# Carries between partitions: from a mended row in DRAM to a product on PE that is added to the gathered run ends, in a four-layer graph network

## The reference

```python
# gat, gatv2, agnn: for each node, over the run of its edges
e = logits(src_features[src], dst_features[dst])
mx = segment_max(e, dst)
ex = exp(e - mx[dst])
out = segment_sum(ex * features[src], dst) / segment_sum(ex, dst)
# cheb0, cheb1: a plain sum over the run
agg = segment_sum((x * Dinv)[src], dst) * Dinv
```

## Time and profile before

| what | us |
|---|---|
| median of 3 runs | 2605.67 (2603.86 to 2609.76) |
| the profiled execution, its time | 2609.88 |
| its span, first to last instruction | 2608.2 |
| PE busy | 1944.9 (75%) |
| DVE busy | 1824.3 (70%) |
| POOL busy | 1740.8 (67%) |
| ACT busy | 894.1 (34%) |

### The profile page before, as it was taken

One profiled execution on the slowest core, in us unless ns is written; L12 is line 12 of the kernel. 1 busy time (PEld: TensorE's weight loads), 2 busy tenths in 40 slices (PEclk: granted clock), 3 DMA queues, 4 the chain that ended last, 5 costly groups with the idle time before them and its releaser, 6 DMA issues.

```text
span 2608.2 us, 51551 instructions
## 1 busy us (share of the span) xinstructions
PE 1944.9 (75%) x20425; PEld 1698.5 (65%) x20425; DVE 1824.3 (70%) x4953; ACT 894.1 (34%) x861; POOL 1740.8 (67%) x1625
## 2 busy tenths in 40 slices
PE   2778775559995399956888956588888888589990
PEld 1778775349995399955888952255555555589990
DVE  7699999145553255542799874488888888599975
ACT  0377765125443154432344534100000000144542
POOL 7777774437775677765667753577777777467773
PEclk7888887569998699975999985699999999799995
DMA  6233332112221122211412213311111111232221
GB/s 234 57 125 124 117 111 89 56 39 65 76 66 35 46 65 77 65 36 50 151 51 64 65 36 143 124 49 50 50 49 50 50 50 47 90 125 65 66 60 21
DMA packets 83703, 194.91 MB, mean 75 GB/s; under 512 B 30960, under 2 KB 49816, under 8 KB 79746
## 3 DMA queue, kind: packets, MB, share of 16 engines
q1 hardware_dynamic: 31650, 139.14, 14.8%
q0 software_dynamic: 51936, 54.27, 10.8%
HBM read 107.92 MB, written 85.39 MB: 74 GB/s over the span
## 4 chain that ended last, share of the span: by engine, by line
POOL 25%; DVE 14%; issue 13%; PE 9%; DMA 2%; ACT 1%; DVEq 0%; POOLq 0%; ACTq 0%
POOL edges_d L600 17%; PE ps L712 7%; POOL rows L600 6%; DVE edges_d L1287 3%; DVE bigT L1354 2%; PE ps L853 2%; POOL starts_dram L603 2%; POOL agg L600 1%; DVE agg L1079 1%; DVE smallT L1079 1%; DVE aggn L1079 1%; DVE prod L1637 1%; DVE logit L1643 1%; DVE prod L1640 1%; DVE rows L1107 1%
## 5 line engine op out<-in xcount | busy, mean ns | idle before, releaser
L712 PE MATMUL ps<-nodes,edges_d 125*128 125x160 bf16 x7140 | 499.4, 234 | 92.4 <-ACT edges_d L895 88.7
L712 PEld LDWEIGHTS ps<-nodes,edges_d 125*128 125x128 bf16 x7140 | 498.2, 98 | 93.7 <-ACT edges_d L895 91.1
L600 POOL DMA_INDIRECT edges_d<-tab_y_dram,attr x425 | 432.1, 1017 | 180.7 <-issue 129.2
L600 POOL DMA_INDIRECT rows<-tab_cheb_dram,src_i x374 | 412.1, 1102 | 174.7 <-issue 112.2
L712 PE MATMUL ps<-nodes,aggn 125*128 125x180 bf16 (+2 forms) x3546 | 395.2, 244 | 122.1 <-DVE rows L1107 63.1
L759 PE MATMUL ps<-edges_d,scan 125*125 125x480 bf16 x1700 | 363.7, 371 | 106.3 <-DVE edges_d L1737 106.3
L1107 DVE COPY_PREDICATED rows<-picks,ps 125x192 f32<-125x192 uint16 (+4 forms) x880 | 353.5, 403 | 82.1 <-issue 41.6
L759 PEld LDWEIGHTS ps<-edges_d,scan 125*125 125x125 bf16 x1700 | 227.8, 137 | 243.2 <-DVE edges_d L1737 110.4
L712 PE MATMUL ps<-nodes,agg 125*128 125x180 bf16 (+2 forms) x3564 | 336.1, 243 | 63.0 <-DVE rows L1107 63.0
L712 PEld LDWEIGHTS ps<-nodes,aggn 125*128 125x128 bf16 x3546 | 292.4, 101 | 128.7 <-DVE rows L1107 62.8
L712 PEld LDWEIGHTS ps<-nodes,agg 125*128 125x128 bf16 x3564 | 283.6, 101 | 68.5 <-DVE rows L1107 54.7
(11 more groups left out here) (334 smaller groups left out, 3146.5 us busy)
## 6 DMA issues: line engine op xcount, KB each, us to landing
src<-srcT_dram SPq DMA_DIRECT2D x70, 437.5 KB
scan_dram<-scan SPq DMA_DIRECT2D x17, 1700.0 KB
scan_dram<-scan SPq DMA_DIRECT2D x34, 425.0 KB
tab_y_dram<-edges_d SPq DMA_DIRECT2D x5, 2880.0 KB, 8.2
scanD_dram<-scan SPq DMA_DIRECT2D x34, 400.0 KB
starts_dram<-scan SPq DMA_DIRECT2D x2, 3400.0 KB, 14.0
edges_d<-tab_y_dram,attr POOLq DMA_INDIRECT x425, 2.6
src<-srcT_dram SPq DMA_DIRECT2D x18, 375.0 KB
```

The source lines that it names most:

```text
L600: pool.indirect_dma_start(o, None, table, bass.IndirectOffsetOnAxis(index, 0)).then_inc(s, SLOT)
L712: ins = pe.matmul(columns_ps[:, i, 0:PICKS * w], hots_[b][lot][:, i * NP:i * NP + P], parts_[:, part, at:at + PICKS * w], start=(lot == 0 ...
```

## The change

The carry no longer goes through DRAM in the four passes with at most one head. In the set-up, each partition's first destination node gets its place among the nodes: `first_row_of` (125x125) is one where the partition's first node lies on that node partition, and only for the first partition of those that begin with the same node; `first_col_of` (125x25) is one in that node's column. At the end of a pass DVE spreads the carry over the 25 columns by a product with `first_col_of` (800 elements in a row in cheb, 25 x 36 = 900 in gatv2 and agnn), and three products on PE with `first_row_of` bring it to the nodes' partitions, into three banks of PSUM. In cheb0 and cheb1 POOL gathers the run ends at once, without `local`, and `block_in` adds PSUM to `agg`. In gatv2 and agnn POOL still gathers `local` first (DVE takes the maximum from it), then gathers the run ends at once; DVE sets two factors per node (`node_keep`), and `block_in` scales the gathered sums and maximum and adds what PE brought, in four instructions. "gat", with four heads, mends its rows in DRAM as before. `no_carry_pq` is computed in each softmax pass, after DVE has released a product on PE, and not in the set-up; the set-up has a further iota on POOL and nine further instructions on DVE.

```diff
...
+    MC = HG + 3
...
+        def mend_rows(c):
+            return tab[0:NP, :, :].rearrange("p j c -> p (j c)")[:, 0:J * c].rearrange("p (j c) -> p j c", c=c)
+
+        def mend_ps(m, c):
+
+            return ps[0:NP, 3 + m // 2, m % 2 * LS * c:(m % 2 + 1) * LS * c].rearrange("p (j c) -> p j c", c=c)
...
+                pool.iota(cross[:, 0:NP], [[1, NP]], base=0, channel_multiplier=0,
+                          allow_small_or_imprecise_dtypes=True).then_inc(consts_made, 1)
+                pool.wait_ge(consts_made, 11)
...
-                    gather(local[:, 0:C], scan_dram, mend_get_i[:, 0:1], local_in)
-                    pool.wait_ge(vec_for_pool, vec_pool.up())
-                    scatter(scan_dram, mend_put_i[:, 0:1], mended[:, 0:C], E - 1)
-                    pool.wait_ge(scattered, put.at())
+                    if heads:
+                        gather(local[:, 0:C], scan_dram, mend_get_i[:, 0:1], local_in)
+                    if heads > 1:
+                        pool.wait_ge(vec_for_pool, vec_pool.up())
+                        scatter(scan_dram, mend_put_i[:, 0:1], mended[:, 0:C], E - 1)
+                        pool.wait_ge(scattered, put.at())
                     for j in range(J):
                         gather(agg[:, j, 0:C], scan_dram, end_i[:, j:j + 1], agg_in[j // LS])
...
+                def carry_to_nodes(c):
+
+                    pe.wait_ge(vec_for_pe, operand.up())
+                    for at in range(0, J, 2 * LS):
+                        n = min(2 * LS, J - at) * c
+                        ins = pe.matmul(ps[0:NP, 3 + at // (2 * LS), 0:n], first_row_of[:, :],
+                                        tab[0:NP, :, :].rearrange("p j c -> p (j c)")[:, at * c:at * c + n],
+                                        start=True, stop=True)
+                    ins.then_inc(pe_for_vec, 1)
...
                         pe.matmul(ps[0:NP, 6, 0:C], carry_qp[:, :], scan[0:NP, 0, (L - 1) * C:L * C],
                                   start=True, stop=True).then_inc(pe_for_vec, 1)
+                        carry_to_nodes(D)
                         return
...
+                    if heads == 1:
+                        carry_to_nodes(MC)
...
-                vec.tensor_scalar(no_carry_pq[:, :], carry_pq[:, :], -1.0, BIG, ALU.add, ALU.mult)
...
+                row_, col_, later = (place_of[:, i:i + 1] for i in range(3))
+                steps = cross[:, 0:NP]
+                again = cross[:, NP:2 * NP]
+                vec.tensor_scalar(row_, ends[:, 0:1], 1.0 / J, -(J // 2) / J, ALU.mult, ALU.add).then_inc(vec_done, 1)
+                settle()
+                vec.tensor_scalar(row_, row_, ROUND, None, ALU.add).then_inc(vec_done, 1)
+                settle()
+                vec.tensor_scalar(row_, row_, -ROUND, None, ALU.add).then_inc(vec_done, 1)
+                settle()
+                vec.scalar_tensor_tensor(col_, row_, -float(J), ends[:, 0:1], ALU.mult, ALU.add).then_inc(vec_done, 1)
+                settle()
+                vec.scalar_tensor_tensor(again, firsts, ends[:, 0:1], before_qp[0:NP, 0:NP], ALU.is_equal, ALU.mult)\
+                    .then_inc(vec_done, 1)
+                settle()
+                vec.tensor_reduce(later, again, X_AXIS, ALU.max).then_inc(vec_done, 1)
+                settle()
+                vec.tensor_scalar(later, later, -1.0, 1.0, ALU.mult, ALU.add).then_inc(vec_done, 1)
+                settle()
+                vec.tensor_scalar(first_row_of[:, :], steps, row_, later, ALU.is_equal, ALU.mult)
+                vec.tensor_scalar(first_col_of[:, :], steps[:, 0:J], col_, None, ALU.is_equal)
...
+                    vec.tensor_scalar(no_carry_pq, carry_pq[:, :], -1.0, BIG, ALU.add, ALU.mult)
...
+                    else:
+                        vec.tensor_copy(mended[0:NP, HG:HG + 1], cross[:, NP:NP + 1])
+                        vec.tensor_copy(mended[0:NP, HG + 1:HG + 2], small[:, 1, 0:1])
+                        vec.memset(mended[0:NP, HG + 2:MC], 1.0).then_inc(vec_for_pe, 1)
                     vec.wait_ge(pe_for_vec, pe_n.up())
                     vec.tensor_copy(crossT[:, 0:heads, :],
                                     ps[0:NP, 7, 0:heads * NP].rearrange("p (h q) -> p h q", h=heads))\
                         .then_inc(vec_for_pe, 1)
                     vec.wait_ge(pe_for_vec, pe_n.up())
+                    agg_n.up(LS * SLOT)
+                    if heads == 1:
+                        vec.tensor_copy(mended[0:NP, 0:HG], ps[0:NP, 6, 0:HG]).then_inc(vec_done, 1)
+                        settle()
+                        carry_to_nodes(mended[0:NP, 0:MC], MC)
+                        for m in range(J // LS):
+                            made = mend_ps(m, MC)
+                            vec.tensor_scalar(node_keep[:, 0, m * LS:(m + 1) * LS], made[:, :, HG + 2], -1.0, 1.0,
+                                              ALU.mult, ALU.add).then_inc(vec_done, 1)
+                        own.up(J // LS - 1)
+                        settle()
+                        for m in range(J // LS):
+                            js = slice(m * LS, (m + 1) * LS)
+                            vec.tensor_tensor(node_keep[:, 1, js], node_keep[:, 0, js], mend_ps(m, MC)[:, :, HG],
+                                              ALU.add).then_inc(vec_done, 1)
+                        own.up(J // LS - 1)
+                        settle()
+                        return
                     vec.tensor_tensor(mended[0:NP, 0:heads * HG], mended[0:NP, 0:heads * HG],
                                       ps[0:NP, 6, 0:heads * HG], ALU.add).then_inc(vec_for_pool, 1)
-                    agg_n.up(LS * SLOT)
-
-                def block_in(m):
+
+                def carry_to_nodes(carry, c):
+
+                    vec.tensor_tensor(mend_rows(c), over(first_col_of[:, :], c),
+                                      carry.unsqueeze(1).broadcast_to([NP, J, c]), ALU.mult).then_inc(vec_for_pe, 1)
+                    vec.wait_ge(pe_for_vec, pe_n.up())
+
+                def block_in(m, heads=None):
 
                     vec.wait_ge(agg_in[m], agg_n.at())
+                    js = slice(m * LS, (m + 1) * LS)
+                    if heads == 0:
+                        vec.tensor_tensor(agg[0:NP, js, 0:D], agg[0:NP, js, 0:D], mend_ps(m, D), ALU.add)\
+                            .then_inc(vec_done, 1)
+                        settle()
+                    if heads == 1:
+                        vec.tensor_tensor(agg[0:NP, js, 0:HG], agg[0:NP, js, 0:HG], over(node_keep[:, 1, js], HG),
+                                          ALU.mult)
+                        vec.tensor_tensor(agg[0:NP, js, HG], agg[0:NP, js, HG], node_keep[:, 0, js], ALU.mult)\
+                            .then_inc(vec_done, 1)
+                        settle()
+                        vec.tensor_tensor(agg[0:NP, js, 0:HG], agg[0:NP, js, 0:HG], mend_ps(m, MC)[:, :, 0:HG], ALU.add)
+                        vec.tensor_tensor(agg[0:NP, js, HG], agg[0:NP, js, HG], mend_ps(m, MC)[:, :, HG + 1], ALU.add)\
+                            .then_inc(vec_done, 1)
+                        settle()
 
                 def finish_sums():
 
                     vec.wait_ge(pe_for_vec, pe_n.up())
-                    vec.wait_ge(local_in, local_n.up(SLOT))
-                    vec.tensor_tensor(mended[0:NP, 0:D], local[0:NP, 0:D], ps[0:NP, 6, 0:D], ALU.add)\
-                        .then_inc(vec_for_pool, 1)
+                    carry_to_nodes(ps[0:NP, 6, 0:D], D)
                     agg_n.up(LS * SLOT)
...
```

More of the change, by code:

```diff
@@ L157, in gnn_kernel @@
         ones = sb("ones", [P, P])
-        shift = sb("shift", [P, P])
         carry_qp = sb("carry_qp", [NP, NP])
         carry_pq = sb("carry_pq", [NP, NP])
-        no_carry_pq = sb("no_carry_pq", [NP, NP])
         ends = sb("ends", [NP, 4])
@@ L197, in gnn_kernel @@
         smallT = sb("smallT", [P, J * NP])
-        before_qp, before_pq = bigT[:, 0:P], bigT[:, P:2 * P]
+        before_qp, before_pq, shift = bigT[:, 0:P], bigT[:, P:2 * P], bigT[:, 2 * P:3 * P]
+        no_carry_pq = cross[:, H * NP + H:H * NP + H + NP]
         tab = sb("tab", [P, J, W0])
@@ L536, in _ @@
                 store_table(tab_fdst_dram, scatf[:, :])
-                run_pass("gatv2", lambda: load_edges(starts32_dram, D, 2 * J + 3))
+                run_pass("gatv2", lambda: load_edges(starts32_dram, D, 2 * J + 1))
                 tile_at, n = {}, 6 * len(GROUPS)
@@ L551, in _ @@
                 store_table(tab_xn_dram, scatf[:, :])
-                run_pass("agnn", lambda: load_edges(starts32_dram, D, 3 * J + 4))
+                run_pass("agnn", lambda: load_edges(starts32_dram, D, 3 * J + 1))
                 for j in range(0, J, LS):
@@ L1452, in softmax_pass @@
                     vec.wait_ge(act_for_vec, act_n.up())
-                    vec.tensor_copy(mended[0:NP, heads * HG:C], small[:, 1, 0:heads])
-                    me = mended[0:NP, 0:heads * HG].rearrange("p (h g) -> p h g", g=HG)
```

(13 more changed lines are left out.)

21 lines of the change are left out of this document (12 added, 9 removed).

## The result

The changed kernel takes 2591.33 us (median of 4 runs) beside 2606.69 for the kernel before, measured with it: 15.4 us less, a ratio of 0.994 (95% interval 0.9928 to 0.9953). A second set gave 2593.29 beside 2610.62, 0.9943 (0.9929 to 0.9957). That lies outside the 0.2% that stand for no change. The forecast was 2588.3, the range 2582 to 2595. The profiled execution took 2592.45 (span 2590.7), where the sum had made 2592.5; its terms are another matter.

A forecast was written before the change was run, and what follows sets the result against it. No engine was full; a chain over all engines bound the kernel, with POOL's gathers or DVE last at pass ends. Gains 11.2 (cheb0, cheb1) + 5.4 (gatv2) + 1.0 (agnn) - 0.2 (set-up) = 17.4 us gave 2588.3, range 2582 to 2595.

The forecast's parts named there:

- The likeliest case: Whole kernel: the summed gains of the pass ends less the set-up, 17.4 us, median 2588.3; chance 0.72.
- The whole shift counts: Rival: gatv2 and agnn hide their added work, so 27.1 us go in all, giving 2578.6; chance 0.05.
- only cheb gains: Rival: the one-head passes' chain is 5 us longer than priced, gatv2 and agnn give nothing, 2594.7; chance 0.05.
- The prices: Costs forecast for the added PE products and DVE instructions, such as 2.8 us for 800-column products and 0.86 per block.
- cheb1's cover: Start of cheb1's block work: DVE's preparation ends at about 1166.0, the first block lands at 1166.9, leaving 0.9 us.
- cheb0, 5.6: End of cheb0: run ends gathered 5.96 us earlier, less 0.36 for one addition; gain 5.60 us.
- gatv2, 5.4: End of gatv2: block 1 reaches ACT 6.4 us earlier, block 3 pays 0.86 more; gain 5.4 us with small stalls.
- The set-up, 0.2: Set-up: nine DVE instructions just about hidden in 2.0 us of idle at landings; loss 0.2 us, at most 1.5.
- The stall rival: Rival: DVE's small instructions stall under POOL's DMA issues, costing 3 us (2591.3), at most 11 (2599.6); chance 0.10.
- The clock rival: Rival: agnn's gather products get less PE clock; at 0.85 about 37 us lost, time 2625; chance 0.08.
- The median: Starting time of the forecast: 2605.67 us for the kernel before, from three runs spread over 6 us.

The follow-up runs named there:

- e2: Changed kernel with the old mending put back in cheb0 and cheb1, new only in gatv2 and agnn; 2604.38 us beside 2608.26, ratio 0.9987.
- e1: Changed kernel with the old mending put back in gatv2 and agnn, new only in cheb0 and cheb1; 2595.81 us beside 2608.26, ratio 0.9953.
- q1: Kernel before with 64 needless waits in GpSimd's program ahead of cheb0's wait for the last store; 2612.09 us, executed once, beside 2603.93.
- q2: Kernel before with 32 tiny unread memsets in VectorE's program in cheb0 ahead of its wait; 2608.95 us, executed once, beside 2603.93.

## Why the prediction was right, point by point

- *The likeliest case* held in every pass: gathers of run ends right behind the store or 1.25 us behind `local`; in gatv2 DVE's chain, not POOL, late next (it reaches block 0 11.09 us after `local`, forecast 1569.3 - 1558.33 = 10.97); in agnn DVE the bound (36.4 us from 2551.73 to 2588.15, forecast 36.7). L881 begins 20.89 us after `local`, 5.97 nearer than before (about 6).
- *The whole shift counts* and *only cheb gains* are out: gatv2 gained about 4 of the 7.60 us and agnn about 1, and the one-head passes alone (e2) 3.9 in the whole time.
- *The prices* held: products of 800 columns 3.03 us (2.8), of 900 3.36 (3.2), the spread 1.10 (1.10), a block's mending 0.87 (0.86), the set-up's nine 2.04 (2.0), cheb1's cover 0.81 (0.9). An addition from PSUM (L1559) and a product of the same shape from SBUF (L1554) took 0.33 both. The Trainium skill, "VectorE: DVE Perf Modes", section "The TRN2 errata", would put 0.06 us between them by its two fixed parts, so the row was right against it.
- *cheb0, 5.6, was mis-sized*: 8.0. The removal of 5.96 and the addition of 0.36 are there; the other 2.4 are the load of GpSimd's program that the kernel before had beside its store, a term that the sum did not have. The 5.02 us between its store and `local`, beside 2.6 in cheb1, stood in the trace, and I had not asked for the difference.
- *gatv2, 5.4, was mis-sized*: 4.4. Block 1 gained 5.98 of 6.4 (5.5 to 5.6 against the three other profiles with the old mending), and block 3 lost 0.72 to the iota. The rule that what is queued behind a moved step moves too was applied to SP's queue and not to POOL's own.
- *The set-up, 0.2*, was nothing, with another cover than the one I named, which a later start of DVE had mostly used up.
- *The stall rival* is a real mechanism, worth about 1 us in gatv2's end (0.25 in block 1, 0.72 in block 3) and not 3; the larger part is the iota's, and not that of DMA issues. *The clock rival*: the granted clock of agnn's pass is 0.98 as before, by the windows over 2273 to 2526.

```profile
2273.00:2526.00 253.00, 243.00 (x3270) 239.32 (x3270) 225.11 (x657) 126.27 (x127) 184.33 (x165) 0.98 0.28 69
```

- *The stretches between* lost 1.6 to 1.75 us in the two profiles of the changed kernel. More than that lies between gatv2's block 3 and agnn's `local`: 959.12 in the one profile of the kernel before, 961.43 and 961.75 after, and 960.0 to 965.0 in the nine variants of either kind that I compared, the one with the old one-head passes (e1) at 963.84 among them. By the letter this is one of the signs of being wrong that the forecast named, a stretch that changes by more than 1 us. But in q1 and q2, which are the kernel before there, the same stretch took 963.44 and 961.49. So it varies by 4.3 us without the change, the one profile of the kernel before is its shortest, and no part of the change is seen in it.
- *The median* was taken from three runs of the kernel before over 6 us; its later sets had 2606.69 to 2610.62, so the gain was 15.4 in one and 17.3 in the other.

## What to carry to other kernels

A shift of a queue shifts everything behind it: list what follows on that queue, and ask what it will run beside. Before a latency is taken from one place, compare it with the same step elsewhere in the trace; a difference (5.0 and 2.6 us here) is a term of its own. And where one engine's chain sets the end, its wait for a group of products can be split: the first block needs only the first.

## What the runs showed of the hardware

- One 0.02 MB load of instructions beside a store held back nine of its 144 packets and delayed the gather behind it by 2.0 to 2.6 us in three kernels (before, e2, q2); with GpSimd's program made longer it came earlier, and the gather 0.6 us late (q1).
- A 125x5 TENSOR_SCALAR on DVE took 0.50 to 1.37 us in place of 0.17 where it met GpSimd's iota of 0.75, TENSOR_TENSORs beside it did not slow; the other way round a GpSimd DMA issue took 1.75 in place of 0.94 beside an 800-element SCALAR_TENSOR_TENSOR, and 1.15 to 1.25 beside the change's own 900-element TENSOR_TENSOR (L1541, gatv2 and agnn in the two profiles of the changed kernel), where DVE's chain hid it. The Trainium skill, "SBUF — State Buffer", section "Who interferes with whom", has a lock that one of the two engines holds for a whole instruction; the stall of TENSOR_SCALAR agrees with it, and TENSOR_TENSOR's freedom beside an iota, which reads no tile, does too.
